# A gated delta-rule layer with a mixture of experts: the output gate as one Silu on ScalarE, and extra products on TensorE at two places of each group

## The reference

```
n = layernorm(x)
q, k, v = split(causal_conv4(n @ qkv_w.T))
z = n @ z_w.T
S = alpha * S ; S += k (v - k S) * beta ; o = q S      # per token and head
o = o * rsqrt(mean(o^2) + 1e-6) * norm_w
o = o * (z * sigmoid(z))                               # the output gate
x = x + o @ out_w.T
x = x + top-2 mixture of 8 experts on layernorm(x)     # router, then relu MLPs
```

## Time and profile before

| what | value |
|---|---|
| median of three runs | 1408.25 us (1407.96 to 1409.8) |
| the profiled execution | 1407.17 us, span 1405.3 us |
| mean granted TensorE clock | 0.933 of full speed |
| busy: PE / DVE / ACT / POOL | 83% / 83% / 59% / 51% |
| chain that ended last | DVE 32%, PE 26%, POOL 16%, issue 10%, DMA 7%, ACT 6% |

### The profile page before, as it was taken

The page is one execution under the profiler, slowest core; times in us unless marked ns, Lnnn a source line. Parts: engine busy times, 40 slices in busy tenths (PEclk is TensorE's granted clock), DMA queues, the critical chain, the costliest instruction groups (busy, mean ns, idle before and its releaser), DMA issues.

```text
span 1405.3 us, 33741 instructions
## 1 busy us (share of the span) xinstructions
PE 1172.5 (83%) x11978; PEld 944.4 (67%) x11978; DVE 1167.0 (83%) x2531; ACT 834.4 (59%) x2536; POOL 710.7 (51%) x598
## 2 busy tenths in 40 slices
PE   0355989898989899898989899999898988469992
PEld 0233868686868686777777777777777777358881
DVE  6878898988888889888888889898989894578875
ACT  1242666665666666666666656566665655348884
POOL 3151726465545555564646373828291914235552
PEclk9996999998989999999999999999999999789996
DMA  6031212222122222222212131313030314332225
GB/s 206 0 98 31 73 36 71 57 59 61 54 62 53 62 54 62 54 61 54 63 52 66 49 69 47 83 35 97 21 99 21 105 18 134 95 105 74 79 64 180
DMA packets 163174, 97.07 MB, mean 69 GB/s; under 512 B 115623, under 2 KB 148269, under 8 KB 161988
## 3 DMA queue, kind: packets, MB, share of 16 engines
q1 hardware_dynamic: 124932, 82.25, 21.5%
q10 hardware_dynamic: 33536, 4.20, 2.1%
q0 software_dynamic: 4544, 8.47, 1.9%
HBM read 73.31 MB, written 24.61 MB: 70 GB/s over the span
## 4 chain that ended last, share of the span: by engine, by line
DVE 32%; PE 26%; POOL 16%; issue 10%; DMA 7%; ACT 6%; SPq 2%; POOLq 0%; DVEq 0%; ACTq 0%
POOL kq L637 9%; DVE Y_sb L1056 7%; DVE blkT L1060 7%; PE kx L1541 3%; POOL decay L629 3%; POOL rows_in L609 2%; DMA blkN<-scr_n 2%; PE kx L1636 2%; POOL kq L620 2%; PE rc L1703 2%; DVE blkN L1047 2%; DVE Gs L1204 1%; DVE area L1146 1%; ACT Gs L836 1%; PE rc L1704 1%
## 5 line engine op out<-in xcount | busy, mean ns | idle before, releaser
L637 POOL TENSOR_TENSOR kq<-tapA,area 128x256 f32<-128x256 f32 x256 | 253.2, 1003 | 89.1 <-DVE area L1146 88.1
L758 ACT ACTIVATE area<-pj,taps 128x256 f32<-128x256 f32 x256 | 123.3, 482 | 138.8 <-PE pj L1555 130.4
L1056 DVE TENSOR_TENSOR Y_sb<-blkT,blkN 128x4 f32<-128x4 f32 (+18 forms) x304 | 172.4, 567 | 10.5
L1541 PE MATMUL kx<-kq 128*128 128x128 f32 x1024 | 143.1, 288 | 43.2 <-ACT area L767 32.6
L609 POOL DMA_INDIRECT rows_in<-rowbuf,dest x64 | 64.8, 1012 | 214.8 <-DVE dest L1132 187.3
L1541 PEld LDWEIGHTS kx<-kq 128*128 128x128 f32 x1024 | 130.2, 199 | 57.8 <-issue 41.2
L1143 DVE SCALAR_TENSOR_TENSOR tapA<-pj,taps,tapA 128x256 f32<-128x256 f32 x256 | 122.2, 477 | 51.7 <-ACT tapA L758 49.8
L620 POOL TENSOR_TENSOR kq<-kq,area 128x1024 f32<-128x1024 f32 x64 | 151.1, 2363 | 0.0
L1060 DVE TENSOR_REDUCE blkT<-Y_sb 128x2 f32<-128x4 f32 (+18 forms) x304 | 142.5, 469 | 5.2
L758 ACT ACTIVATE tapA<-pj,taps 128x256 f32<-128x256 f32 x256 | 123.1, 481 | 0.0
L1146 DVE SCALAR_TENSOR_TENSOR area<-pj,taps,area 128x256 f32<-128x256 f32 x256 | 121.4, 474 | 0.0
(11 more groups left out here) (305 smaller groups left out, 3593.6 us busy)
## 6 DMA issues: line engine op xcount, KB each, us to landing
area<-scr_alpha SPq DMA_DIRECT2D x32, 512.0 KB, 4.2
area<-scr_acum SPq DMA_DIRECT2D x32, 512.0 KB, 3.8
blkN<-scr_n SPq DMA_DIRECT2D x32, 256.0 KB, 4.3
area<-rows_in SPq DMA_DIRECT2D x39, 130.0 KB, 2.2
scr_n<-area SPq DMA_DIRECT2D x128, 32.0 KB, 1.6
area<-rows_out SPq DMA_DIRECT2D x4, 1024.0 KB, 8.0
rows_in<-rows_in SPq DMA_DIRECT2D x8, 260.0 KB, 3.8
kq<-in_x SPq DMA_DIRECT2D x4, 512.0 KB, 6.0
```

The lines of the kernel that those rows point to most:

```text
L637: nc.gpsimd.tensor_tensor(dst[:, n % H, :], tapA[:, n % RING, :], tapB[:, n % RING, :], ALU.add).then_inc(conv_done, 1)
L758: ins = nc.scalar.activation(dst[:, n % RING, :], pj[n % 2][:, k:k + GT], ACT.Copy, scale=taps[:, t, k:k + 1])
L1056: ins = nc.vector.tensor_tensor(p4, bc(blkT[:, r0:, j:].rearrange("p r (o m) -> p r o m", o=1), [128, nr, w, wd]), bc(blkN[:, j:j + w, j:] ...
L1541: ins = mm(o, lhs[:, hh, cs], rhs_[:, hh, cs], start=True, stop=True)
```

## The change

1. ScalarE applies Silu to z, scaled by 1 / WSCALE, and writes the finished gate. VectorE's step `zg` is gone (the words `zg` stay in the list and nobody acts on them), and `ow` carries the missing factors. The bank of z is now given back by ScalarE (`zg_ready` is raised by `zt`).
2. Since VectorE's order no longer protects `zg` from being overwritten, `zt` waits for `g_ready` of the same half.
3. In each call that has both g and a, TensorE runs seven products of 128 x 512 (f16) ahead of `kq.0.1` and eight ahead of `gt.0.0`. They write `pj[0]`, which is free there; nobody reads them before `z.0.0` overwrites the bank. Before each set TensorE waits for the bank as `z.0.0` does.

```
-                        act.wait_ge(z_mm, halves(a, c, u))
-                        nc.scalar.activation(zg[:, c, HU * u:HU * u + HU, :], heads(pj[u]), ACT.Tanh,
-                                             scale=0.5 / WSCALE).then_inc(z_tanh, 1)
+                        if g is not None:
+                            act.wait_ge(g_ready, halves(g, c, u))
+                        act.wait_ge(z_mm, halves(a, c, u))
+                        nc.scalar.activation(zg[:, c, HU * u:HU * u + HU, :], heads(pj[u]), ACT.Silu,
+                                             scale=1.0 / WSCALE).then_inc(zg_ready, 1)
...
-            nc.vector.tensor_scalar(ow[:, :, :], ow[:, :, :], nw[:, 0:1], 0.5 / WSCALE / VSCALE, ALU.mult,
+            nc.vector.tensor_scalar(ow[:, :, :], ow[:, :, :], nw[:, 0:1], 1.0 / VSCALE, ALU.mult,
...
-                    elif step == "zg":
-
-                        c, u = arg
-                        dve.wait_ge(z_tanh, halves(a, c, u))
-                        nc.vector.scalar_tensor_tensor(out=half(zg, c, u), in0=half(zg, c, u), scalar=1.0,
-                                                       in1=heads(pj[u]), op0=ALU.add, op1=ALU.mult).then_inc(zg_ready, 1)
...
+            STAND_INS = {
+                ("kq", 0, 1): (("z", 0, 0), pj[0], 7),
+                ("gt", 0, 0): (("z", 0, 0), pj[0], 8),
+            }
...
+            def stand_in(step, g, a, r):
+
+                use, bank, n = STAND_INS[step]
+                bank_free(use, g, a, r)
+                for _ in range(n):
+                    mm(bank[:, :], wv_hi[:, 0, 0:C], wv_hi[:, 0, 0:512], start=True, stop=True)
...
                 for step, *arg in STEPS:
+                    if g is not None and a is not None and (step, *arg) in STAND_INS:
+                        stand_in((step, *arg), g, a, r)
```

More of the change, by code:

```diff
@@ L197, in preln_delta_moe_kernel @@
         (diag_ready, decay_done, kk_ready, n_ready, ktr_ready, kd_ready, scale_ready, kq_ready, at_ready,
-         ka_ready, aq_ready, z_mm, z_tanh, zg_ready) = sems(
+         ka_ready, aq_ready, z_mm, zg_ready) = sems(
             "diag_ready decay_done kk_ready n_ready ktr_ready kd_ready scale_ready kq_ready at_ready ka_ready "
-            "aq_ready z_mm z_tanh zg_ready")
+            "aq_ready z_mm zg_ready")
         (blk_in, inv_step, inv_done, t_out, t_in, rdiag) = sems("blk_in inv_step inv_done t_out t_in rdiag")
@@ L705, in _ @@
                 nc.scalar.activation(wv_hi[:, k, :], wv_taps[k], ACT.Copy, scale=-VSCALE).then_inc(s_vhi, 1)
-            for t in (z_tanh, kd_ready, rhs_ready, u_ready, sq_done, gn_ready, gt_ready):
+            for t in (zg_ready, kd_ready, rhs_ready, u_ready, sq_done, gn_ready, gt_ready):
                 act.sem_inc(t, HALVES)
@@ L1015, in _ @@
             dve.wait_ge(s_zero, 1)
-            for t in (n_ready, at_ready, zg_ready, S_ready, g_ready):
+            for t in (n_ready, at_ready, S_ready, g_ready):
                 dve.sem_inc(t, HALVES)
```

## The result

The changed kernel takes 1418.02 us (median of 9 runs, 1407.98 to 1424.24) against 1409.8 us (9 runs, 1407.89 to 1413.31) for the kernel before on the same chip: ratio 1.0059, 95% interval 1.0031 to 1.0088. 1387 and "faster" were forecast. The profiled execution took 1414.97 us, its span is 1413.0 against 1405.3. From the page after: the span, the busy shares, the granted clock in 40 slices, and the queue that brings TensorE's program.

The account below looks back on a forecast made before the run. Each group was a circle: VectorE decides up to dest, then GpSimd's late start, then TensorE. 1407.17 - 12.6 - 10.95 + 0 + 2.8 = 1386.4 us against the profiled execution, stated as 1387; range 1376 to 1400.

Parts of the forecast that it names:

- Part 3: Stand-ins ahead of kq.0.1 and gt.0.0 keep TensorE's clock full, closing VectorE's waits for router logits: 10.95 us less.
- C: Rival: the clock falls despite the stand-ins, which stick out 1 us before gt.0.0 in fourteen groups: 1410 us; chance 0.05.
- Part 1: VectorE's gate instructions leave; dest comes 1.19 us sooner, 0.97 reaches the call's end in thirteen groups: 12.6 us less.
- Part 2: Gate on ScalarE: Silu lasts as long as tanh, a table load costs 0.6 us, about 0.6 won back; together 0.
- The bank of z comes free from ScalarE sooner than it did from VectorE: TensorE's wait behind the inversion: about 0.6 us won once, in the first call.
- part 1's second pair: VectorE's two gate instructions behind st.1.0: removing them only lengthens a wait for ScalarE; counted 0, not below 0.
- What may be given back: Half clock behind TensorE's wait for the inverted blocks, in two more groups at 1.4 us: 2.8 us more.
- Rival D: Half clock behind the wait for the blocks in nearly every group, 2.8 us each: slower, 1421 us; chance 0.04.
- does not move: The inversion's result going out and back, ahead of ScalarE's first taps, was taken to keep its time.

Follow-up runs that it names:

- after_pe_held: The whole changed kernel plus one wait: TensorE starts z.1.0 only when VectorE has done x2.1; ratio 0.9876 to the kernel before.
- standins_only: The kernel before with only TensorE's stand-in products added, tanh and VectorE's gate step zg kept; ratio 0.9893 to the kernel before.
- after_held: The changed kernel with GpSimd held back by 24 semaphore increments between dest and its first scatter; ratio 1.0054 to the kernel before.
- standins_again: The kernel before with only the stand-in products added, the same kernel as standins_only timed again; ratio 0.9906 to the kernel before.

## Why the prediction was wrong

By its own steps:

- **Part 3**, 10.95 us in 14 gaps: right, and a little too low. From the start to the end of an inversion a group takes 30.51 us where it took 31.50, 12.8 us in 13 groups. The clock stays full there, the cover was as forecast, C did not happen. The Trainium skill, page "TensorE: Matmul & The Clock Gate", section "Part 4: PE-mode transpose", says that transposes do not count as other products do. The 15 ordinary products a group that brought the windows above from 0.51 to 1.00 fit that, but do not test it: they also fill waits in which TensorE stood idle.
- **Part 1**, `dest` 1.19 us sooner: right; it stands 0.41 us behind E and was at 1.60 (677.31 in the earlier trace rows). That 0.97 of it reaches the next inversion is nearly so where nothing disturbs it: the five clean groups gain 36.97 - 36.13 = 0.84 us, after_pe_held 0.61 over all 13.
- **Part 2**: the Silu takes 0.59 to 0.60 us as the tanh did, and each table load 1.28 us, as the row of before had it. A switch with 2.66 us, as the Trainium skill, page "ScalarE: Activation LUTs", section "What ACT_TABLE_LOAD costs", has it with its drain, can't be told from these rows.

```profile
L785 ACT ACT_TABLE_LOAD x1 | 1.3, 1283 | 0.0
L904 ACT ACT_TABLE_LOAD x1 | 1.3, 1283 | 0.0
```

- **The step that failed** stands in part 2: "The bank of z comes free from ScalarE sooner than it did from VectorE", counted as harmless, and with it part 1's second pair "I count 0 ... not below 0". VectorE's gate was what kept TensorE back behind the inversion. Without it TensorE has nothing new to do and reaches `proj.2` 0.9 us before its bank is free, and its queue is 1.2 us further on just behind E. Two prices hang on that earliness: the half clock behind the wait, and the late landings. Taking it away again (after_pe_held) gives back 25 us of the 13 groups (894.9 on that chip, 869.9), and these 869.9 are 20.2 less than before's 890.1 (from another chip, where the changed kernel has 893.6), where parts 1 and 3 promised 13 x (0.97 + 0.78) = 22.75.
- **"What may be given back"**, two more groups at 1.4 us, 2.8 in all: the mechanism was seen, the size was not. Seven more groups were cold. Of the eight, three without a late landing cost 38.28 - 36.13 = 2.15 us each, and five with one 40.29 - 36.13 = 4.16 each, together 27.3 us. Rival D (2.8 us in each of thirteen groups, chance 0.04) is nearest to what happened, 1418.02 against its 1421, but it came near in part by luck: it had neither the late landings nor the last call. Its argument against, "one group of fourteen now", was drawn from a kernel in which TensorE came later.
- **The late landing** was in no rival. Part 1 held that the way of the inverted blocks out and back "does not move". It moved by 1.0 to 1.5 us in five of 13 groups. That the packet of TensorE's program does it is inferred from the 42 cases.
- **The last call** (+6.0 us) was counted at nothing and is not explained.

## What to carry to other kernels

An instruction that is taken off one engine may have been the brake of another: list who waited for it, follow each of them to its next wait, and ask what clock and which transfers are there. A half-clock stretch costs by where it lies: some 7 us at half clock ahead of the row numbers, in all 13 groups, hid for all but about 1 us (standins_only has groups of 67.4 us, before of 68.5). Against that, 3.4 us at half clock behind the wait for the blocks cost 2.15. Where an engine can't use its earliness, holding it back can pay, as the one wait of after_pe_held did.

## What the runs showed of the hardware

- TensorE's program comes in packets of 16 KB, by the counts above one for 256 instructions, on a queue of its own. The 42 packets behind E took 0.9 to 1.7 us each. Where one started 0.7 to 2.9 us behind E, at which a transfer of many small rows is issued (128 KB in rows of 128 bytes), that transfer landed 0.7 to 1.7 us late, 42 times in 42; starting at 3.2 us it did no harm.
- The same program does not meet its fetches alike in every run: late landings were 5, 3 and 4 of 13 in three traces of the changed kernel, and its times spread over 1.1% (1407.98 to 1424.24) where before's spread over 0.4%.
- The wait itself is not all that decides about the clock: after_held waits 0.8 us at `proj.2` in each group like after, and has 2 cold groups, not 8. What differs there is that GpSimd comes later; why that keeps the clock up is open. In standins_again 4 groups are cold without a wait at `proj.2`.
- Semaphore increments take time: 24 of them held GpSimd back by 1.9 us (the first scatter stands at E + 3.55 in place of E + 1.67), 0.08 us each.
